# A decoder layer on one core: high and low parts of queries and keys kept in DRAM, their stacks loaded by GpSimd's transfers

## The reference

```python
x = x + attn(layernorm(x))      # 32 query heads, 8 key/value heads of 32, causal, rotary
x = x + xattn(layernorm(x), ctx)  # both operands rounded to 0..255 steps, then a product
x = x + ffn(layernorm(x))       # base product, plus a low-rank part of 8 experts weighed by a softmax

def attn(x):
    q, k, v = split(x @ w_qkv.T + b_qkv)
    q, k = apply_rope(q), apply_rope(k)
    scores = where(causal, q @ k.T / sqrt(32), -1e20)   # per head, 512 x 512
    return (softmax(scores) @ v) @ w_o.T + b_o
```

## Time and profile before

| | |
|---|---|
| median of three runs | 812.7 us |
| the profiled execution | 808.7 us, span of its instructions 806.9 us |
| granted TensorE clock, mean | 0.936 |
| busy: PE, DVE, ACT, POOL | 692.1, 439.8, 475.0, 404.4 us |
| transfers | 88.26 MB, all but instructions on SP's queue; 34.8% of the 16 engines |

### The profile page before, as it was taken

One profiled execution on the slowest core, in us unless ns is written; L12 is line 12 of the kernel. 1 busy time (PEld: TensorE's weight loads), 2 busy tenths in 40 slices (PEclk: granted clock), 3 DMA queues, 4 the chain that ended last, 5 costly groups with the idle time before them and its releaser, 6 DMA issues.

```text
span 806.9 us, 13270 instructions
## 1 busy us (share of the span) xinstructions
PE 692.1 (86%) x4580; PEld 553.2 (69%) x4580; DVE 439.8 (55%) x1047; ACT 475.0 (59%) x1113; POOL 404.4 (50%) x496
## 2 busy tenths in 40 slices
PE   4988699999999899886578678899989776599998
PEld 3887578887767677664355456678867555488886
DVE  4245376787777775575656655535224666721112
ACT  4225589989887786778675766657313761522320
POOL 5248766635765731446651730415624757844430
PEclk9998899999999999998678699999999988989999
DMA  8405655434446341402221221302335144243202
GB/s 280 181 6 152 202 176 164 130 100 132 128 124 196 105 137 50 145 31 90 90 85 43 63 79 33 108 35 89 121 105 170 62 141 136 66 143 105 66 10 95
DMA packets 52897, 88.26 MB, mean 109 GB/s; under 512 B 6368, under 2 KB 14944, under 8 KB 52832
## 3 DMA queue, kind: packets, MB, share of 16 engines
q1 hardware_dynamic: 52832, 87.43, 34.8%
HBM read 72.72 MB, written 9.44 MB: 102 GB/s over the span
## 4 chain that ended last, share of the span: by engine, by line
PE 54%; POOL 14%; DVE 11%; ACT 10%; issue 7%; DMA 3%; SPq 0%; DVEq 0%; ACTq 0%; POOLq 0%
PE dense L1036 35%; PE probt L933 6%; PE score L921 4%; PE pv L948 4%; POOL w_lo L1600 4%; ACT prob_all L1141 2%; POOL ln_s L1583 2%; PE score L1036 2%; DVE q_stack L1289 2%; POOL ln_s L1585 2%; DVE prob_all L1305 1%; POOL ctx_add L1619 1%; POOL prob_all L1631 1%; DVE stats L1349 1%; ACT q_stack L1126 1%
## 5 line engine op out<-in xcount | busy, mean ns | idle before, releaser
L1036 PE MATMUL dense<-w_hi,act_t 128*128 128x512 f32 (+1 forms) x740 | 248.9, 400 | 26.6 <-DVE act_t L1365 12.4
L1600 POOL TENSOR_TENSOR w_lo<-stage,w_hi 128x512 fp32r<-128x512 f32 x89 | 117.1, 1325 | 138.6 <-ACT w_hi L1077 138.3
L1141 ACT ACTIVATE prob_all<-prob_all,neg_max 128x128 f32<-128x128 f32 (+3 forms) x256 | 142.6, 557 | 74.7 <-DVE neg_max L1305 73.0
L1305 DVE CUSTOM_DVE_ANT_0 prob_all<-score,mask_sb 128x128 f32<-128x128 f32 (+3 forms) x256 | 122.8, 484 | 112.5 <-PE score L921 111.7
L1036 PEld LDWEIGHTS dense<-w_hi,act_t 128*128 128x128 f32 x740 | 142.4, 198 | 57.6 <-POOL w_lo L1600 16.2
L1036 PE MATMUL dense<-w_lo,act_t 128*128 128x512 f32 (+1 forms) x400 | 150.2, 395 | 6.3 <-ACT w_lo L1082 3.2
L1036 PE MATMUL dense<-act_t,w_hi 128*128 128x512 f32 x392 | 137.5, 433 | 1.0 <-DVE w_lo L1273 1.0
L933 PE MATMUL probt<-ident_sb,prob_all 128*128 128x128 f32 x640 | 117.5, 284 | 0.9 <-DVE prob_all L1314 0.6
L921 PE MATMUL score<-k_stack,q_stack 96*128 96x128 f32 (+3 forms) x256 | 93.5, 370 | 22.4 <-DVE neg_max L1305 16.0
L933 PEld LDWEIGHTS probt<-ident_sb,prob_all 128*128 128x128 f32 x640 | 83.5, 147 | 16.5 <-issue 2.7
L1077 ACT ACTIVATE w_hi<-stage 128x512 fp32r<-128x512 f32 x117 | 72.2, 623 | 36.9 <-PE dense L1036 16.9
(11 more groups left out here) (145 smaller groups left out, 1008.7 us busy)
## 6 DMA issues: line engine op xcount, KB each, us to landing
q_stage<-rope_dram SPq DMA_DIRECT2D x64, 192.0 KB, 3.1
stage<-in_w_qk SPq DMA_DIRECT2D x40, 256.0 KB, 2.9
stage<-in_w_o SPq DMA_DIRECT2D x32, 256.0 KB, 3.0
stage<-in_ctx_kv SPq DMA_DIRECT2D x24, 256.0 KB, 3.1
stage<-in_w_org SPq DMA_DIRECT2D x24, 256.0 KB, 2.8
rope_dram<-xres SPq DMA_DIRECT2D x20, 256.0 KB, 2.6
xres<-in_x SPq DMA_DIRECT2D x8, 512.0 KB, 4.9
prob_all<-in_x SPq DMA_DIRECT2D x8, 512.0 KB, 6.4
```

The costliest lines, as they stand in the source:

```text
L1036: last = engine.matmul(dst, lhs, rhs, start=(k == 0 and c == 0), stop=(k == g.kts - 1 and c == len(pairs) - 1))
L1141: engine.activation(prob[:, u % P_SLOTS, 0:length], prob[:, u % P_SLOTS, 0:length], ACT.Exp, bias=neg_max[:, m:m + 1], scale=-1.0, accum_o ...
L1305: engine.tensor_tensor_reduce(prob[:, u % P_SLOTS, 0:length], score_bank[u % 2][:, 0:length], mask_sb[:, S - length:S], -1.0, HIGHEST, ALU ...
L1600: engine.tensor_tensor(slot_lo(p, 0, NW), raw_of(p), slot_hi(p, 0, NW).bitcast(F32), ALU.subtract).then_inc(g_piece, 1)
```

## The change

The split into high and low part is done once per rotated tile, before it is stored, instead of once per stack. ACT copies the rotated tile of 128 x 512 into a free place of `act_t` as float32r (`rope_high`), POOL subtracts that from the tile in place (`rope_low`), and SP stores three planes per job in `rope_dram`: twice the high part and once the low part, in the order of the terms. Each group then needs two transfers, which POOL issues: 192 KB of keys and 768 KB of queries straight into `k_stack` and `q_stack`, which both now have two sets. The staging tiles, the table of factors, ACT's and DVE's work per stack and SP's loads are gone. The store of a job comes later (13.5 us of the planner's time after the tile is whole, 9.0 us for the first three jobs, before 7.0), and with it the reload of x and the bias adds. The tail has five more weight slots instead of three.

```diff
-TAIL_W_SLOTS = 3
+TAIL_W_SLOTS = 5
...
-SPLIT_LAG = 4
+EARLY_LAGS = 6.5, 7.5, 9.0, 13.0
+ROPE_LAGS = 10.0, 12.0, 13.5, 18.0
...
-        q_stage = sb("q_stage", [TERMS * HD, NT, GROUP * P])
-        k_stage = sb("k_stage", [TERMS * HD, S])
-        q_stack = sb("q_stack", [P, NT, GROUP * P], F32R)
+        q_stack = sb("q_stack", [P, 2, GROUP, S], F32R)
         k_stack = sb("k_stack", [P, 2, S], F32R)
...
-        rope_dram = nc.dram_tensor("rope_dram", [ROPES, P * S], F32, kind="Internal").ap()
+        rope_dram = nc.dram_tensor("rope_dram", [ROPES, TERMS, P, S], F32, kind="Internal").ap()
...
+            high = act_t[ATTN_T[plan.ropes[m][1]]][:, m % 2, KD - 1 - m // 2 % 2, :]
...
-            rope_out_at.setdefault(plan.after(j, 7.0), []).append(m)
+            high, low, put, load = EARLY_LAGS if m < 3 else ROPE_LAGS
+            rope_high_at.setdefault(plan.after(j, high), []).append(m)
+            rope_low_at.setdefault(plan.after(j, low), []).append(m)
+            rope_out_at.setdefault(plan.after(j, put), []).append(m)
+            loadable[m] = plan.after(j, load)
...
-        load_at = {}
+        load_at, latest = {}, 0
         for gi in range(GROUPS):
...
+            b, g = divmod(gi, NKV)
+            jobs = plan.rope_no["q", b, g], plan.rope_no["k", b, g // GROUP]
+            free = first_unit + NT * GROUP * (gi - 1) + 2 if gi > 1 else 0
+            latest = max(latest, free, *(loadable[m] for m in jobs))
+            load_at.setdefault(latest, []).append(gi)
...
             def put_roped(m):
...
+                r, done = rope_space(m), d_roped[m % ROPE_SLOTS]
+                low = 1 if plan.ropes[m][0] == "k" else 2
+                e.wait_ge(a_rhi, m + 1)
+                for term in range(TERMS):
+                    if term != low:
+                        engine.dma_start(rope_dram[m, term], r["high"].bitcast(F32)).then_inc(done, 16)
+                e.wait_ge(g_rlo, m + 1)
+                engine.dma_start(rope_dram[m, low], r["raw"]).then_inc(done, 16)
...
-            def load_keys(gi):
...
-            def load_queries(gi, i):
...
             def score(u):
                 gi, i, h = unit(u)
                 length = (i + 1) * P
-                e.wait_ge(v_klo, gi + 1)
-                e.wait_ge(v_qlo, NT * gi + i + 1)
+                e.wait_ge(d_kstack[gi % 2], 16 * (gi // 2 + 1))
+                e.wait_ge(d_qstack[gi % 2], 16 * (gi // 2 + 1))
...
-            def queries_high(gi, i):
...
-            def keys_high(gi):
...
+            def rope_high(m):
+                r = rope_space(m)
+                e.wait_ge(g_add, m + 1)
+                engine.activation(r["high"], r["raw"], ACT.Copy).then_inc(a_rhi, 1)
...
-            def queries_low(gi, i):
...
-            def keys_low(gi):
...
+            def rope_low(m):
+                r = rope_space(m)
+                e.wait_ge(a_rhi, m + 1)
+                engine.tensor_tensor(r["raw"].bitcast(F32R), r["raw"], r["high"].bitcast(F32), ALU.subtract).then_inc(g_rlo, 1)
+
+            def load_stacks(gi):
+                b, g = divmod(gi, NKV)
+                mk, mq = plan.rope_no["k", b, g // GROUP], plan.rope_no["q", b, g]
+                if gi >= 2:
+                    e.wait_ge(t_score, last_unit(gi - 2) + 1)
+                e.wait_ge(*roped(mk))
+                rows = rope_dram[mk].rearrange("a (r h) c -> h r a c", h=GROUP)[g % GROUP]
+                engine.dma_start(k_stack[0:TERMS * HD, gi % 2, :], rows.bitcast(F32R)).then_inc(d_kstack[gi % 2], 16)
+                e.wait_ge(*roped(mq))
+                rows = rope_dram[mq].rearrange("a (r h) c -> r a (h c)", h=GROUP)
+                engine.dma_start(q_stack[0:TERMS * HD, gi % 2, :, :].rearrange("p h c -> p (h c)"),
+                                 rows.bitcast(F32R)).then_inc(d_qstack[gi % 2], 16)
...
                 for m in rope_add_at.get(j, ()):
                     add_swapped(m)
+                for m in rope_low_at.get(j, ()):
+                    rope_low(m)
+                for gi in load_at.get(j, ()):
+                    load_stacks(gi)
```

## The result

The changed kernel takes 831.85 us (median of 4 runs, 829.97 to 833.62) where the kernel before took 810.75 us (4 runs, 808.59 to 814.67). The ratio is 1.0254 with a 95% interval of 1.0202 to 1.0307: 2.5% slower. The forecast was 808.2 us with a range of 789 to 824, so the time lies outside. Executions more than 1.5% above their kernel's fastest (at most two of a kernel, one of them in e12 at 1637.49 us) are left out of the times and ratios of the experiments, and as the profiled executions of e12 and e14 are of this kind, only the start is read from these two.

A forecast was written before the change was run, and what follows sets the result against it. PE was taken to bound 95.5 to 223 and 277 to 331 us, a chain through fixed-order engines 223 to 277 and 331 to 534. Gains of 17 us less costs of 12.5 gave 812.7 - 4.5 = 808.2 us, range 789 to 824.

The forecast's parts named there:

- what comes: Added work: 20 copies on ACT, 12.5 us; on POOL 20 subtractions, 26.5 us, and 32 issues, 32 us.
- late weight pieces: Risk if POOL's added work is no longer covered by other work; costed at 0.
- The traffic term: 10 MB more traffic on 88, with the DMA share at 0.50 at most; costed at 0.
- Stretches where PE is full: 95.5 to 223 and 277 to 331 us: PE sets the pace, so removing splits wins 2 us (0 to 4).
- 223 to 277 us: Stretch with 5.5 us of splits on the chain and 6.7 us of idle PE; 4 us won (2 to 7).
- 331 to 534 us: Stretch where no engine is full, 5.5 to 15.7 us of splits on the chain; 10 us won (3 to 18).
- rival A: Fixed order gives back more: 25 us won from 331 to 534 us, 6 from 223 to 277; 791 us, chance 0.25.
- The start: First score at 105.0 us, 9.5 us later, behind POOL's subtractions, two issues and a 6.3 us landing of 768 KB.
- The clock term: At the start, the longer pause may lengthen the 1.2 GHz stretch at the restart; 1 us lost (0 to 2).
- The bias add: Fourth bias add ends at 331.9 us, so DVE's take-out waits 5.1 us; cost 2 us (0 to 5.1).
- The tail: Two more weight slots let ACT and POOL make pieces earlier; 1 us won (-3 to 4).
- B: Rival: POOL's transfers are slow, over 13.3 us for issue and landing, so group 1 waits; 823 us, chance 0.2.

The follow-up runs named there:

- e12: e10 with the copies of the first three jobs on ACT and those of later jobs on POOL; 796.05 us, 0.9835 of before.
- e14: e12 with the first group's query load cut into four transfers of 48 KB and four of 144 KB; 797.29 us, 0.9846 of before.
- e3: The kernel before with only the 20 copies on ACT added, read by nobody, all splits kept; 822.87 us, 1.0203 of before.
- e1: The changed kernel with the copy that makes the high part moved from ACT to POOL; 821.96 us, 1.019 of before.
- e5: The changed kernel with the stack loads of groups 2 to 15 issued three units later; 820.04 us, 1.0105 of before.
- e10: e9 with the copy on POOL instead of ACT; 798.00 us, 0.9851 of before.
- e9: The changed kernel with stack loads three units later, 3 tail slots, and earlier steps for the first three and last four jobs; 809.93 us, 1.0009 of before.
- e6: The changed kernel with the copy on POOL, 3 tail slots, copy and subtraction right behind the addition, and earlier stores; 836.64 us, 1.0307 of before.
- e4: The changed kernel with the tail's extra weight slots set back from 5 to 3; 823.70 us, 1.0211 of before.
- e8: e6 with the stack loads issued by SP instead of POOL; 816.57 us, 1.0062 of before.
- e11: e9 with the stack loads issued by SP; 805.95 us, 0.9956 of before.
- e13: e12 with the stack loads issued by SP; 792.78 us, 0.9809 of before.

## Why the prediction was wrong

**The step that failed** is the one on what comes: the 20 copies of ACT were priced as "12.5 us" of work and then got no term in the sum; POOL's part was called "beside other work", and late weight pieces were the only risk that I named. The copy was counted as work and not as a wait: I did not ask whom it waits for, nor what stands behind it on ACT. In the kernel before only SP and POOL waited for the rotation; POOL stood 21.2 us in 10 places for swaps, while PE idled 0.8 us in groups 0 to 5. The copy ties ACT's exponentials to POOL's addition, to SP's swap, and to the traffic of the stack loads. It waited 32.3 us in 12 places, and the bias additions behind the stores another 8.0 us in 3. e3 shows that the copy alone is dear (15.5 us on the kernel before), e1 and e5 show the wait in groups 1 and 2, and e10 beside e9 shows it in group 8. The traffic term, "10 MB on 88" put at 0, failed with it: the share of the DMA engines was low, but two 128 KB swaps that start with a 960 KB load land in 4.4 and 7.3 us, not 2.3. The trace of the kernel before had a sign of it that I did not read: its two swaps of 128 KB at 252 us, issued 2 to 3 us behind three 512 KB reloads of x, took 5.0 and 5.3 us.

**Stretches where PE is full.** Forecast: 2 us won. Measured: 14.4 us lost over groups 0 to 5 and 7.2 over groups 8 and 9, 21.6 in all, most of it by the above. With these waits gone, e10 needs 127.7 us against 127.8 and 53.7 against 53.9. Nothing is won there, at the lower bound of the term.

**223 to 277 us.** Forecast 4 us won (2 to 7), measured 4.9 in groups 6 and 7, and 9.0 in e10, above the range and above the 6.7 us that PE idled before: the granted clock rose too, from 0.94 to 1.00. The 4.9 still hold ACT's waits for stores of group 7, 1.3 and 3.5 us, so part of the agreement is luck.

**331 to 534 us.** Forecast 10 us (3 to 18), measured 7.3 in groups 10 to 14, and 11.4 in e10. PE idle there is 44.2 us, near the 40 announced, against 50.6. The step was right; rival A's 25 us did not come.

**The start.** Forecast 9.5 us later plus 1 for the clock, first score at 105.0; measured 11.0 us later, at 106.43, PE's wait released by the transfer of q_stack as announced. Its parts:

```profile
98.03 0.71 POOL L1513 DMA_DIRECT2D k_stack<-rope_dram  x1
98.76 0.52 POOL L1516 DMA_DIRECT2D q_stack<-rope_dram  x1
```

and on PE:

```profile
106.43 0.66 PE L895 MATMUL score<-k_stack,q_stack 96*128 96x128 f32 x2 [15.52 <-DMA q_stack<-rope_dram]
```

POOL stands at the loads at 98.03, not 96.7; an issue takes 0.5 to 0.7 us, not 1.0; and the 768 KB take 7.7 us instead of 6.3, so the errors partly cancel. The clock term was in the wrong place: the stretch at 1.2 GHz went on for 5.3 us behind the first score, against 4.7 before, and it was in groups 1 and 2 that PE's waits were followed by the low clock, at 5.0 us. The Trainium skill (DMA: Bandwidth & Descriptors, the anatomy of one DMA on the GpSimd path) would give 3.8 us for this transfer; the median here is 7.7 us (5.9 to 9.9), and the measurement decides.

**The bias add.** Forecast: 2 us. DVE's take-out of the fourth tile waits 4.6 us for it, as announced (5.1):

```profile
356.87 0.69 DVE L1352 TENSOR_TENSOR xres<-dense,xres 128x512 f32<-128x512 f32 x1 [4.58 <-POOL xres L1587]
```

Group 9, in which it lies, lost 1.6 us and got them back in e6 to e10, where the planned order has this addition earlier.

**The tail.** Forecast: 1 us won (-3 to 4). Measured: 4.6 us lost, and e4 shows that the two slots do it. The step had said that norms and sums keep their slots; PE's first product on the sum over the context did not.

**The rivals.** B named the right side and came nearer (823 us), but by luck: its mechanism did not happen; no later group waits for a stack (PE's only wait for q_stack is the first), and loads land in 9.9 us or less against its 13.3. The queries' loads landed in 6.7 to 7.3 us (medians of e8, e11 and e13) when SP issued them, so POOL's path, with 6.9 to 7.7, was not slow either. It shares with the truth only that the loads matter, through what they delay.

## What to carry to other kernels

An instruction that is added to an engine with a fixed order can cost its wait on top of its duration, and more: write down for each added instruction whom it waits for, whether that producer had slack that nobody saw, and what stands behind it, before its duration. A large transfer is best placed away from a small one that somebody waits for; the mean share of the DMA engines doesn't show this. And a saving in one form can hide behind a constant of the same change: here 3 instead of 5 slots, the load three units later, stores up to 3 us earlier for seven jobs and the copy on POOL turned 2.5% slower into 1.5% faster than before (e10), with the splits still gone.

## What was not expected of the hardware

- A transfer of 128 KB within SBUF lands in 2.3 us alone; two of them took 4.4 and 7.3 us when 960 KB were issued in the same microsecond on another queue, and 6.4 and 7.6 us when the 960 KB were issued 1.5 to 2 us ahead of them on the same queue (e8).
- 768 KB from DRAM took 6.9 to 7.7 us to land (medians) when POOL issued them and 6.7 to 7.3 when SP did; 192 KB took 3.9 us in the changed kernel. An issue by POOL occupied it for 0.5 to 0.7 us.
- 20 copies of 0.63 us, 12 of them after a wait, on an engine that was busy 59% of the span made a kernel 15.5 us slower (e3).
